# Node tiles loaded and normalised ahead of the adjacency strips, a reordered first step, and one fp32 copy of W0 in a two-layer graph kernel

## The reference

```python
# layer 0
HW = einsum('bnf,fo->bno', relu(layernorm(x)), W0)
A_norm = relu((A + A.T) * 0.5);  D = sum(A_norm, axis=1)
d = where(D > 0, D_safe ** -0.5, 0)
x = x + relu(einsum('nm,bmo->bno', eye(N) - d[:, None] * A_norm * d[None, :], HW))
# layer 1
h = einsum('bjf,kfo->kbjo', relu(layernorm(x)), W)          # three products
x = x + diag(adj) @ h[0] + triu(adj, 1) @ h[1] + tril(adj, -1) @ h[2] + bias
```

## Time and profile before

| | us |
|---|---|
| median of 3 runs (lowest, highest) | 968.15 (968.04, 968.94) |
| the profiled execution | 966.95 |
| its span on the core | 965.1 |
| PE busy in the span | 915.6 (95%) |
| DVE busy | 554.6 (57%) |
| ACT busy | 493.7 (51%) |
| POOL busy | 283.9 (29%) |

### The profile page before, as it was taken

One profiled execution on the slowest core, in us unless ns is written; L12 is line 12 of the kernel. 1 busy time (PEld: TensorE's weight loads), 2 busy tenths in 40 slices (PEclk: granted clock), 3 DMA queues, 4 the chain that ended last, 5 costly groups with the idle time before them and its releaser, 6 DMA issues.

```text
span 965.1 us, 17388 instructions
## 1 busy us (share of the span) xinstructions
PE 915.6 (95%) x4535; PEld 774.2 (80%) x4535; DVE 554.6 (57%) x1481; ACT 493.7 (51%) x1042; POOL 283.9 (29%) x284
## 2 busy tenths in 40 slices
PE   3657999999999999999999998999999999999998
PEld 2547788888888888888888887888888888888886
DVE  4896787777777776565656554543433433433442
ACT  2898466666666664555455554343333333333331
POOL 4783344344343443434434442111111100000000
PEclk9899999999999999999999999999999999999999
DMA  9996999999999985655565555676656655555552
GB/s 286 328 265 156 290 338 322 326 327 332 324 331 318 335 275 180 178 171 162 174 196 161 166 175 176 187 221 190 188 179 189 193 160 170 166 164 165 158 168 69
DMA packets 181689, 213.73 MB, mean 221 GB/s; under 512 B 13712, under 2 KB 116112, under 8 KB 179600
## 3 DMA queue, kind: packets, MB, share of 16 engines
q1 hardware_dynamic: 138928, 159.23, 54.6%
q10 hardware_dynamic: 42720, 54.01, 16.1%
HBM read 145.04 MB, written 68.16 MB: 221 GB/s over the span
## 4 chain that ended last, share of the span: by engine, by line
PE 88%; DVE 4%; ACT 2%; SPq 2%; DMA 1%; issue 1%; POOL 0%; DVEq 0%; ACTq 0%; POOLq 0%
PE psAcc L543 24%; PE psAcc L541 24%; PE psAcc L542 24%; PE psA L427 3%; PE psG L510 2%; PE psG L512 2%; PE psG L511 2%; PE psZ L469 2%; DVE sring L842 1%; DMA colb<-in_adj 1%; ACT hst L573 1%; SPq L236 1%; PE psW L396 1%; DVE n_st L797 1%; PE psW L395 1%
## 5 line engine op out<-in xcount | busy, mean ns | idle before, releaser
L607 ACT ACTIVATE Lh<-C 128x512 fp32r<-128x512 f32 x256 | 161.3, 631 | 293.4 <-PE psAcc L543 233.0
L541 PE MATMUL psAcc<-Xh,Lh 128*128 128x512 f32 x512 | 206.1, 402 | 0.7 <-DVE Xl L975 0.4
L541 PE MATMUL psAcc<-Yh,Lh 128*128 128x512 f32 x512 | 200.8, 392 | 0.0
L543 PE MATMUL psAcc<-Xh,Ll 128*128 128x512 f32 x512 | 200.7, 392 | 0.0
L542 PE MATMUL psAcc<-Xl,Lh 128*128 128x512 f32 x512 | 200.2, 391 | 0.0
L543 PE MATMUL psAcc<-Yh,Ll 128*128 128x512 f32 x512 | 200.1, 391 | 0.0
L542 PE MATMUL psAcc<-Yl,Lh 128*128 128x512 f32 x512 | 199.9, 390 | 0.0
L784 DVE TENSOR_TENSOR Ll<-C,Lh 128x512 fp32r<-128x512 f32 x128 | 90.8, 711 | 143.8 <-ACT Lh L607 143.7
L543 PEld LDWEIGHTS psAcc<-Xh,Ll 128*128 128x128 f32 x512 | 96.3, 188 | 20.8
L543 PEld LDWEIGHTS psAcc<-Yh,Ll 128*128 128x128 f32 x512 | 96.1, 188 | 20.3
L541 PEld LDWEIGHTS psAcc<-Xh,Lh 128*128 128x128 f32 x512 | 96.6, 189 | 18.8 <-issue 1.5
(11 more groups left out here) (125 smaller groups left out, 1380.4 us busy)
## 6 DMA issues: line engine op xcount, KB each, us to landing
C<-at_dram SPq DMA_DIRECT2D x128, 256.0 KB, 2.7
at_dram<-AT SPq DMA_DIRECT2D x16, 1088.0 KB, 5.5
R<-in_adj SPq DMA_DIRECT2D x64, 256.0 KB, 6.2
C<-in_adj SPq DMA_DIRECT2D x64, 256.0 KB, 5.2
s_dram<-C ACTq DMA_DIRECT2D x64, 256.0 KB, 5.0
g_dram<-g ACTq DMA_DIRECT2D x32, 512.0 KB, 3.6
C<-s_dram SPq DMA_DIRECT2D x64, 256.0 KB, 3.9
t_dram<-x ACTq DMA_DIRECT2D x32, 256.0 KB, 2.1
```

The lines of the kernel that those rows point to most:

```text
L541: mm(acc, lh, rh[:, kd, :], start=k == 0, stop=False)
L543: mm(acc, ll, rh[:, kd, :], start=False, stop=c < L1 and k == NB - 1).then_inc(used, 1)
L607: A(Lh[:, q, :], C[:, q, :], ACT.Relu if s.c < L1 else ACT.Copy).then_inc(lhi, 1)
```

## The change

Four things are changed together.

1. SP loads the first four node tiles between the parts of strip 15, then the weights (which were the very first transfer), and then three tiles ahead of each of the strips 14, 13 and 12, two ahead of 11 and one ahead of 10. The waits of PE, ACT and DVE for the weights stay at the head of their queues.
2. The steps of the node tiles get new places by chunk number: several tiles' statistics, normalisations and turns stand behind the same chunk (3, 7, 11, 15, 18). The turned tile is written back to its own place in `hst` and the products rotate through three PSUM buffers.
3. The work at the end of the first stage is moved forward into the chunk loop, or (products of tiles 13 to 15, last transpose of `R`) into step 0. SP loads the first two quarters of R and C earlier. In step 0 the turn of `xp` stands behind the last matmul.
4. W0 has one fp32 copy (`W0`), and the turned tile of the steps one fp32 copy (`yTs`). `by_W0` makes one fp32 matmul for each block. `Wh` and `Wl` hold layer 1's weights only.

```diff
-        TILES_WITH = [2, 2, 2, 2, 1, 2, 1, 1, 2, 1, 0, 0, 0, 0, 0, 0]
+        TILES_WITH = [0, 3, 3, 3, 2, 1, 0, 0, 0, 0, 0, 0, 0, 0, 0, 0]
...
+        NORMAL_AT = [1, 1, 3, 3, 3, 3, 7, 7, 7, 7, 11, 11, 15, 15, 18, 18]
...
-            return psZ[:, :] if j == 12 else psW[:, :] if j == 13 else psG[:, j % 2, :]
+            return psAcc[:, 1, :] if j == NB - 1 else psZ[:, :] if j % 3 == 2 else psG[:, j % 3, :]
...
-            x1w = x1[:, 0, :]
-            sp.dma_start(x1w[:, 0:F], w_l0).then_inc(ld_w, 16)
-            sp.dma_start(x1w[:, F:4 * F].rearrange("p (k o) -> p k o", k=3),
-                         w_l1.rearrange("k f o -> f k o")).then_inc(ld_w, 16)
+            def load_weights():
+                sp.dma_start(W0[:, :], w_l0).then_inc(ld_w, 16)
+                sp.dma_start(x1[:, 0, 0:3 * F].rearrange("p (k o) -> p k o", k=3),
+                             w_l1.rearrange("k f o -> f k o")).then_inc(ld_w, 16)
+
...
+                    load_tiles([g])
                     sp.dma_start(rowb[:, 0, c], rows_v[k, :, c]).then_inc(ld_first[g], 16)
...
-                    if g < TILES_WITH[0]:
-                        load_tiles([g])
+                load_weights()
...
-                if i == NB - 5:
-                    load_next(Step(None, 0), 0)
-            for q in range(1, NQ):
+                if i in (10, 12):
+                    load_next(Step(None, 0), i // 2 - 5)
+            for q in range(2, NQ):
                 load_next(Step(None, 0), q)
...
-            def by_W0(dst, hi, lo):
+            def by_W0(dst, src):
                 for b in range(HB):
                     f = slice(b * F, (b + 1) * F)
-                    mm(dst[:, f], hi[:, f], Wh[:, 0:F], start=True, stop=False)
-                    mm(dst[:, f], hi[:, f], Wl[:, 0:F], start=False, stop=False)
-                    last = mm(dst[:, f], lo[:, f], Wh[:, 0:F], start=False, stop=True)
+                    last = mm(dst[:, f], src[:, f], W0[:, :], start=True, stop=True)
                 return last
...
-                for b in range(HB):
-                    f = slice(b * F, (b + 1) * F)
-                    last = mm(product0(j)[:, f], T0[j % 4][:, f], x1[:, 0, 0:F], start=True, stop=True)
-                last.then_inc(w0_ok, 1)
+                if j < NB - 1:
+                    wait(pe, prep_hi, j - 2)
+                    wait(pe, prep_lo, j - 2)
+                by_W0(product0(j), hst[:, node(j), :]).then_inc(w0_ok, 1)
...
+                if n in (36, 39):
+                    pe.wait_ge(at_ok, 1 if n == 36 else 2)
...
-                if k == 11 and c < NB:
-                    if c == 0:
-                        pe.wait_ge(prep_hi, 13)
-                        pe.wait_ge(prep_lo, 13)
+                if k == (11 if c else 15) and c < NB:
...
+                    if c == 0 and q == 0:
+                        pe.wait_ge(p0S, len(CH0))
+                        rows_T(t, 3)
+                        times_W0(13)
+                        times_W0(14)
+                        times_W0(15)
...
-            A(Wh[:, :], x1[:, 0, :], ACT.Copy).then_inc(whi_ok, 1)
+            A(Wh[:, :], x1[:, 0, 0:3 * F], ACT.Copy).then_inc(whi_ok, 1)
...
-                wait(act, w0_ok, j - 3)
-                A(T0[j % 4], psAcc[:, j % 2, :], ACT.Copy).then_inc(t0_ok, 1)
+                A(hst[:, node(j), :], psAcc[:, j % 2, :], ACT.Copy).then_inc(t0_ok, 1)
...
-                    A(yTh[:, :], psZ[:, :], ACT.Copy).then_inc(yThi, 1)
+                    A(yTs[:, :], psZ[:, :], ACT.Copy).then_inc(yT_ok, 1)
...
-                if c < NB:
-                    wait(dve, yThi, t.of(1, 1))
-                    V.tensor_tensor(yTl[:, :], psZ[:, :], yTh[:, :].bitcast(F32), ALU.subtract).then_inc(yTlo, 1)
```

More of the change, by code:

```diff
@@ L448, in _ @@
                         columns0(e)
+                for j in range(len(TIMES_AT)):
+                    if TIMES_AT[j] == n:
+                        times_W0(j)
                 for j in range(NB):
@@ L485, in finish @@
                     if c <= NB:
-                        wait(pe, yThi, t.of(1, 0))
-                        wait(pe, yTlo, t.of(1, 0))
+                        wait(pe, yT_ok, t.of(1, 0))
                     wait(pe, hThi, t.of(1, -2))
@@ L827, in degrees, with stats_at @@
                                        op0=ALU.mult, op1=ALU.add).then_inc(d_safe, 1)
+            def stats_at(n):
+                for j in range(NB):
+                    if STAT_AT[j] == n:
+                        stats0(j)
+                        for u in range(NB // 2):
+                            if MEAN_AFTER[u] == j:
+                                mean0(u)
             def scaled_lo(j):
@@ L1018, in _ @@
                     added[g] = ADDS0[n + 1] + 1
+                for e in range(len(ROOT_AT)):
+                    if ROOT_AT[e] == n:
+                        root(e)
                 for u in range(NB // 2):
-                    if 4 * u + 2 == n:
+                    if POWER_AT[u] == n:
                         pool.wait_ge(s0_ve, u + 1)
                         power(n0s[u % 3].rs[:, :], n0s[u % 3].ve[:, :], mhalf[:, 0:2 * HB]).then_inc(s0_rs, 1)
-                for e in range(len(DEG_AT)):
-                    if DEG_AT[e] - 1 == n:
-                        root(e)
             root(len(GROUPS) - 1)
```

134 lines of the change are left out of this document (58 added, 76 removed).

## The result

The changed kernel is slower. Its time is 992.9 us (median of 4 runs, 990.8 to 994.4), against 968.1 us (965.6 to 968.9) of the kernel before on the same chip: a ratio of 1.0256, with a 95% interval of 1.0235 to 1.0277. The forecast was 982.0 us in a range of 970 to 992. The sign was right; the loss was 24.8 us where 13.9 were forecast, and the time lies just above the range.

What follows compares the result with a forecast made beforehand. Bound: the engines' common progress over 40 chunks, then PE from 110 us on. Chunk 39 27.7 us later, less 7.4 (stage end), less 6.4 (product): +13.9 on 966.95, 980.9; 982 as median, range 970 to 992.

Steps and rivals of the forecast that it cites:

- The bound: PE has no idle time from 110 us on; before step 0 the four engines' common progress over 40 chunks sets the pace.
- The walk: First stage, four queues followed chunk by chunk: late weights and bursts put chunk 39 at about 111.5 us, 27.7 us later.
- The product: W0 product in steps 1 to 16: 1.29 us falls to 0.89, 0.40 us saved a step, 6.4 us in all.
- The rival of dearer fp32 products: W0 products in the steps cost more than in the first stage, +7.5 instead of -6.4 us: 996 us; chance 0.03.
- The late start: Start of the first stage: weights behind four tiles and strip 15 land at about 15 us, so work starts 8 us late.
- The rival of early weights (977): Weights land soon after issue (8 us), so the first stage moves by 5 us: +9, 977 us; chance 0.12.
- The bound at chunk 39: End of the first stage: chunk 39's delay lies between 18 and 37 us, giving +4 to +23, 972 to 991 us.
- POOL is then the longest: From chunk 22 (86 us) POOL sets the pace: 18.4 us of adds and roots from 91.5, chunk 39 at about 111.5.
- The end of the stage: Reordered end and step 0: step 1 starts 18.3 us behind chunk 39 instead of 25.7, 7.4 us gained.
- which drops the 2.34 us wait: In step 0, turning xp behind the last matmul removes PE's 2.34 us wait at 105.50 us.
- The bursts overlap: Rival: DVE runs ahead while ACT normalises, chunk 39 stays at 84 to 88 us: about -12, 956 us; chance 0.11.
- A further stall: Rival: strips fetched late, as loads wait for bunched sums, or R landing after chunk 39: above 991 us; chance 0.07.

Runs made afterwards that it cites:

- the product alone: Kernel before with only the fp32 W0 product of steps 1 to 16 changed, first stage as before: 961.3 us, ratio 0.9929.
- half of the adds: Changed kernel with POOL adding only the first half of each chunk's columns to the column sums: 987.0 us, ratio 1.0207.
- The runs with the old stage and the new end: Changed kernel with weights, tile loads and tile steps in old order: 962.8 us; that kernel with R's transposes out of the chunk loop again: 964.5 us.
- the spread-out kernel: Changed kernel with weights loaded first and tile steps spread out, at most one tile's statistics behind a chunk: 974.5 us, ratio 1.0083.
- the loads alone: Kernel before with node tiles loaded ahead of the strips as in the change, weights first, all steps at old chunks: 973.4 us, ratio 1.0064.

## Why the prediction was right and wrong

**The bound.** Right but for the steps 1 and 2, in which PE waits 3.1 us: what counts is the start of step 1 and the work on PE after it. The chain of cause that the prediction named (late weights, bursts in which ACT and DVE wait in turn) is what the traces and the runs show, but it is only half of it. Of the 36 us at chunk 39, 18 are the late weights and the bunching; the other 18 stay when both are undone, and are the tiles' loads and steps standing ahead of the chunks, with some of the new end's ties (see below). The walk had put all of them under the weights and the bursts.

**The product.** Right: 6.4 us forecast, 6.6 in the profile, 6.9 by the ratio of the product alone. The rival of dearer fp32 products is out: four products are eight records in 1.05 us by the row, 0.89 us of PE's time as forecast. The Trainium skill ("FP8 and Floating Point Precision", TensorE Precision Notes) gives true FP32 four passes through the array. The prediction took each record for a pass, and nothing in the traces shows that. A matmul of 512 columns starts 0.23 us behind the last one in these steps, so a quarter of it is 0.06 us for 128 columns, and a product of 128 columns in fp32 takes 0.22 us, about four times that (an estimate from these rows). In time the trace is in line with the page. It doesn't prove it, since a product of 128 columns in fp32r also takes 0.11 us, twice the quarter; three of those cost more than one in fp32.

**The late start.** Right in size: 15 us forecast for the weights, 14.71 measured; 8 us forecast, 8.0 at chunk 39 by the run with the weights first. The rival of early weights (977) is out. That the same 8 us cost nothing in the old order, the prediction had left unsaid.

**The walk.** This is the step that failed: the term for the delay at chunk 39 was mis-sized, 27.7 us in the sum and 36.35 measured. It was near up to chunk 19, with what had been forecast first: chunk 4 at 36.9 (35), chunk 8 at 52.8 (50.5), chunk 12 at 63.0 (61.3), chunk 16 at 74.9 (72.4), chunk 19 at 86.6 (83.6). The bound at chunk 39 was 18 to 37 us late, and 36.35 was measured against the forecast 27.7. It was short by 8.65 us:

- 3.0 us had gathered by chunk 19, as small waits in each burst.
- 5.0 us between the chunks 19 and 22, which took 7.4 us (86.6 to 94.0) where the walk had 2.4 (83.6 to 86). It had forgotten the turns of the tiles 14 and 15 in the last round, which stand ahead of chunk 21 on PE and wait for ACT (5.08 us at 88.95). The run with these turns later shows that the gap is hardly a term by itself: without it DVE and ACT are late instead, and chunk 39 gains 0.5 us.
- 0.65 us from chunk 22 to 39, 26.14 us against 25.5. "POOL is then the longest" was the walk's reason, and by the run with half of the adds POOL alone does not set this length: right length, unproved cause.

**The end of the stage.** The size was right up to step 1 (138.69 is 18.5 us behind chunk 39, forecast 18.3, before 25.7: 7.2 us gained of 7.4). But this is no gain on top of an unchanged chunk 39: in the old order the new end delays chunk 39 by 5.8 us (89.1 against 83.3), and brings step 1 forward by 1.0 only. Wrong was also the term "which drops the 2.34 us wait" as a gain that stays. Waits of 3.1 us came in the steps 1 and 2, with a stretch at a clock of 0.88 behind them, about 5 us together, for which the sum had no term. Ahead of the turn of step 2 the chain begins with the transfer that took 8.6 us, in DVE's timeline of the changed kernel:

```profile
160.19 0.87 DVE L747 BATCH_NORM_STATS2 np_st<-xp 128x6 f32<-128x128 f32 x4 [2.31 <-DMA xp<-in_x]
```

The prediction had said it would be wrong "if PE shows idle time in steps 1 to 16", and it does. The runs with the old stage and the new end show the price free of the rest: 962.8 and 964.5 us against 961.3 for the product alone. The reordering has no net gain.

**What the 36 us are made of**, by the runs, each read at chunk 39: the late weights 8.0 (120.2 to 112.2), the bunching 10.2 (112.2 to 102.0), the tiles loaded ahead of the strips 5.1 (88.9 against 83.8, in the old order), and 13.1 for having the tiles' steps ahead of the chunks at all (102.0 against 88.9). The last figure is a difference of two kernels, not an experiment of its own. It assumes that the loads cost the same in both, and it holds the ties of the new end as well, which only the spread-out kernel has: from chunk 35 to 39 it takes 9.2 us, the loads alone 7.6. Its shape says how it comes about. At chunk 4 the spread-out kernel (24.8 us) is level with the loads alone (25.2); at chunk 19 it is 16.2 us behind (68.3 and 52.1); at chunk 39 it is 13.1 behind. The stretches up to chunk 19, of the spread-out kernel and then of the loads alone, show the work in them:

```profile
0.00:68.00 68.00, 33.34 (x169) 27.84 (x169) 41.94 (x174) 43.62 (x112) 37.36 (x37) 0.83 0.87 251
...
0.00:52.00 52.00, 22.17 (x121) 18.07 (x122) 27.90 (x110) 25.82 (x68) 28.65 (x31) 0.93 1.05 304
```

Up to chunk 19 ACT has 17.8 us and DVE 14.0 us more to do, for a delay of 16.2 us: work that was taken out of the last third and put into the first two delays them by about its own length on ACT. It gives only 3.1 us back. The changed kernel shows the same: from chunk 22 to 39 it takes 26.1 us, the product alone 31.6, for a third that no longer holds any tile's statistics or normalisation.

**The rivals.** "The bursts overlap" (956) had its test at chunk 8 before 32 us; it came at 52.8. "A further stall" above 991, at 0.07, named the time that came (992.9) but not the cause: the loads of the strips did stand still (16 GB/s from 50 to 60 us), as that rival said (each load waits for the sums three strips back, not two), but from the weights' landing up to 94 us no idle time of PE ends with a strip's transfer. Behind it three do, for 2.7 us together (0.95 at 102.60, 0.18 at 105.96, 1.59 at 109.29). Up to chunk 22 the stalled loads followed from the late sums, and did not cause them. The bound of 37 us at chunk 39 was nearly met (36.35) and by itself gave 991. The range's end of 992 left 1 us above it, and there was no term at all for what the moved turn of `xp` could cost.

## What to carry to other kernels

Where several engines work in fixed program order on a common list of chunks, put side work evenly between the chunks, and put it where the cover is: a burst makes each engine wait for the other in turn, which cost 10 us here. Work that is moved ahead of the chunks delays them even when it is spread evenly (13 us here, with 17.8 us more of ACT's work up to chunk 19), and what it frees later may be taken by another limit. A late start or a wait has no price of its own; it costs what the order behind it can't cover, so test the same delay in both orders (here nothing in one and 8 us in the other). A wait that is "dropped" by moving its instruction back has to be looked for in the next two or three steps before it is counted as a gain, and so has a gain behind a point to be looked for as a loss ahead of it.
